# Routing of a mixture of experts: the last tile ahead of the 0/1 products, picks ahead of the destinations, the second half's picks in two pieces

## What is computed

```python
xf = x.reshape(T, D)                       # T = 1024 rows, D = 512, after a layer norm
logits = xf @ gate_w.T                     # 8 experts
probs = softmax(logits)
top_p, top_i = top_k(probs, 2)
w = top_p / (sum(top_p) + 1e-09)
capacity = int(1.25 * T / 8)               # 160 rows of each of the two choices per expert
oh = one_hot(top_i, 8)
rank = cumsum(oh, axis=0) - 1
keep = sum(rank * oh, -1) < capacity
comb = einsum('tk,tke->te', w * keep, oh)
for e in range(8):
    y = (silu(xf @ gate_proj_w[e].T) * (xf @ up_proj_w[e].T)) @ down_proj_w[e].T
    out = out + comb[:, e:e+1] * y
```

## Time and profile before

| what | us |
|---|---|
| median of 3 runs | 1009.5 |
| lowest and highest run | 1008.39, 1009.78 |
| the profiled execution | 1006.8 |
| its span, first to last instruction | 1005.1 |

### The profile page before, as it was taken

How to read it: one execution, slowest core, us unless ns; L and a number is a source line. 1 busy time by engine, 2 the same in 40 slices (tenths; PEclk the granted TensorE clock), 3 DMA queues, 4 the chain that set the end, 5 groups by cost and what they waited for, 6 DMA issues and landing times.

```text
span 1005.1 us, 14411 instructions
## 1 busy us (share of the span) xinstructions
PE 985.9 (98%) x5412; PEld 777.0 (77%) x5412; DVE 614.8 (61%) x1142; ACT 393.7 (39%) x631; POOL 215.9 (21%) x202
## 2 busy tenths in 40 slices
PE   7999999999999999999999999899999999999998
PEld 4886444445454468878888887899999999999997
DVE  6368443344655565896466668577665666656666
ACT  3332211222111143355667542444544444445441
POOL 2053400002000036454422124720000000000051
PEclk9999999999999999999999999999999999999999
DMA  9809599999999922033311100885764756645543
GB/s 295 317 1 381 241 361 417 409 414 397 415 396 408 388 94 74 1 92 108 110 42 38 32 1 7 277 283 156 217 188 151 206 159 196 189 155 183 152 150 133
DMA packets 45959, 206.91 MB, mean 206 GB/s; under 512 B 5760, under 2 KB 16256, under 8 KB 41680
## 3 DMA queue, kind: packets, MB, share of 16 engines
q1 hardware_dynamic: 40256, 187.95, 52.6%
q0 software_dynamic: 5648, 18.22, 5.4%
HBM read 190.04 MB, written 16.12 MB: 205 GB/s over the span
## 4 chain that ended last, share of the span: by engine, by line
PE 85%; DVE 7%; DMA 6%; issue 1%; ACT 0%; SPq 0%; POOL 0%; DVEq 0%; ACTq 0%
PE ps L486 59%; PE ps L621 7%; PE ps L650 7%; DMA big<-in_ctxT 3%; DMA big<-in_ctx 2%; DVE stats L1315 2%; PE ps L480 2%; PE ps L598 1%; PE ps L951 1%; PE ps L856 1%; PE ps L978 1%; PE ps L654 1%; PE ps L631 1%; PE ps L493 1%; DVE hr L1324 1%; PE ps L532 1%
## 5 line engine op out<-in xcount | busy, mean ns | idle before, releaser
L486 PE MATMUL ps<-x,w 128*128 128x320 f32 x1536 | 235.6, 309 | 0.0
L486 PEld LDWEIGHTS ps<-x,w 128*128 128x128 f32 x1536 | 228.0, 188 | 0.4
L1839 DVE TENSOR_TENSOR w<-big,w 128x1536 fp32r<-128x1536 f32 x64 | 112.1, 1753 | 78.3 <-ACT w L1249 78.3
L486 PE MATMUL ps<-hsplit,w 128*128 128x320 f32 x672 | 107.7, 309 | 0.0
L1249 ACT CAST w<-big 128x1536 fp32r<-128x1536 f32 x64 | 94.2, 1475 | 29.2 <-PE ps L486 27.0
L486 PEld LDWEIGHTS ps<-hsplit,w 128*128 128x128 f32 x672 | 100.8, 188 | 0.1
L486 PE MATMUL ps<-xcT,u 128*128 128x512 f32 x432 | 98.2, 389 | 0.0
L621 PE MATMUL ps<-big 128*64 128x512 f32 (+2 forms) x512 | 95.9, 500 | 0.7 <-DVE s_stat L1495 0.6
L486 PEld LDWEIGHTS ps<-xcT,u 128*128 128x128 f32 x432 | 81.0, 188 | 17.0 <-DVE xcT L1627 0.2
L650 PE MATMUL ps<-big 128*64 128x512 f32 x384 | 86.4, 597 | 1.7 <-DMA big<-in_ctx 1.5
L621 PEld LDWEIGHTS ps<-big 128*64 128x64 f32 x512 | 44.2, 136 | 51.0 <-issue 39.1
(11 more groups left out here) (336 smaller groups left out, 1544.6 us busy)
## 6 DMA issues: line engine op xcount, KB each, us to landing
big<-in_ctxT SPq DMA_DIRECT2D x16, 3202.0 KB, 19.3
big<-in_ctx SPq DMA_DIRECT2D x16, 3072.0 KB
big<-in_w_units SPq DMA_DIRECT2D x64, 768.0 KB, 4.4
big<-in_dense_units SPq DMA_DIRECT2D x41, 256.0 KB, 2.7
xs<-big POOLq DMA_DIRECT2D x1, 5120.0 KB, 17.4
big<-in_gate_units SPq DMA_DIRECT2D x12, 384.0 KB, 3.0
hr<-xs SPq DMA_DIRECT2D x28, 160.0 KB, 5.8
ys<-big POOLq DMA_DIRECT2D x28, 160.0 KB, 5.6
```

The lines of the kernel that those rows point to most:

```text
L486: mm = nc.tensor.matmul(dst, lhs[x], rhs[w], start=start and x + w == 0, stop=stop and x == 1)
L1839: V.tensor_tensor(wsplit[f % RING][1][:], wraw[f % RING], wsplit[f % RING][0][:].bitcast(F32), ALU.subtract).then_inc(w_low, 1)
```

## The change

PE's order behind the last output chunk changes: the first quarter of the first half's rows goes ahead of tile 5's logits; tile 6's logits, and `ranks_before`, go behind the transposition of tile 7; tile 7's logits follow tile 6's at once. The second half's products are made in two rounds over the four quarters, tiles 4 and 5 in the first, 6 and 7 in the second, instead of all four tiles for each quarter.

On DVE the slot within the first expert no longer comes out of `scat`'s chain: `one_hot` adds one sum (L1747 of the new file, `rt[:, 7]`), `positions` ends with one sum of the rank and that (`rt[:, 1]`), and the picks compare with it. The four instructions that lead to `scat` are a function `destinations` of their own behind the picks. The cut at the capacity isn't in the picks' numbers; a rank over the capacity gives a number that no slot of its choice has. The second half's picks are two instructions of two tiles each. `one_hot(0)` moves ahead of tile 5's `last_apply`. On ACT the last two instructions of the stretch change places.

```diff
-            def first_expert_rows(d, h):
-                pe.wait_ge(picked, h + 1)
-                if h == 0:
+            def first_expert_rows(d, q):
+                pe.wait_ge(picked, q + 1)
+                if q == 0:
                     wait_bank_free(pe, "gx", d)
-                for i in range(4 * h, 4 * h + 4):
+                for i in range(*((0, 4), (4, 6), (6, 8))[q]):
                     pe.wait_ge(row_low, i + 1)
...
-                if h:
+                if q == 2:
                     mm.then_inc(xt_done if d else gx_done, 1)
...
             output_chunks(7, 5, HC)
+            first_expert_rows(0, 0)
             logits(1, 5, 4, 6)
-            first_expert_rows(0, 0)
             transposed_tiles(6, 7)
-            ranks_before()
-            logits(1, 6, 4, 6)
             first_expert_rows(1, 0)
             transposed_tiles(7, 8)
+            logits(1, 6, 4, 6)
+            logits(2, 7, 7, 7)
             first_expert_rows(2, 0)
-            logits(2, 7, 7, 7)
+            ranks_before()
+            ranks_within(1)
             first_expert_rows(3, 0)
-            ranks_within(1)
-            for d in range(DC):
-                first_expert_rows(d, 1)
+            for q in (1, 2):
+                for d in range(DC):
+                    first_expert_rows(d, q)
...
             last_transposed(6)
+            last_transposed(7)
             rows_high(7)
-            last_transposed(7)
...
+                rt_chained(V.tensor_tensor(rt[:, 7, n], rt[:, 2, n], slot_at[:, 1, n], ALU.add))
...
                 rt_chained(V.tensor_reduce(rt[:, 3, n], rk[:, n, :], AX_X, ALU.add))
+                rt_chained(V.tensor_tensor(rt[:, 1, n], rt[:, 3, n], rt[:, 7, n], ALU.add))
+
+            def destinations(h):
+                _, n = half_tiles(h)
                 rt_chained(V.tensor_tensor(rt[:, 5, n], rt[:, 3, n], rt[:, 2, n], ALU.add))
...
             choose(0, 0, 4)
+            one_hot(0)
             last_apply(5)
-            one_hot(0)
             last_norm(6)
             positions(0)
             last_apply(6)
             dve.wait_ge(slots_in, 16)
-            pick_rows(0)
+            pick_rows(0, 4)
+            destinations(0)
             last_norm(7)
             last_apply(7)
             choose(1, 4, 7)
             choose(2, 7, 8)
             one_hot(1)
             positions(1)
-            pick_rows(1)
+            pick_rows(4, 6)
+            pick_rows(6, 8)
+            destinations(1)
```

More of the change, by code:

```diff
@@ L958, in transpose_picks @@
             def transpose_picks(i):
-                pe.wait_ge(picked, 3 + NT // 2)
+                pe.wait_ge(picked, 4 + NT // 2)
                 if i == 0:
@@ L1759, in positions, with pick_rows @@
                 V.tensor_copy(scat[:, n], rt[:, 4, n]).then_inc(idx_done, 1)
[L1761 to L1765, removed]
+            def pick_rows(lo, hi):
+                ids = slot_ids.rearrange("p (k s) -> p k s", s=CAP).unsqueeze(1).to_broadcast([P, hi - lo, TOPK, CAP])
+                V.tensor_tensor(pick[:, lo:hi, :].rearrange("p i (k s) -> p i k s", s=CAP), ids,
+                                r3[1][:, lo:hi, :].unsqueeze(3).to_broadcast([P, hi - lo, TOPK, CAP]),
                                 ALU.is_equal).then_inc(picked, 1)
```

## The result

The changed kernel takes 1003.91 us (median of 5 runs, 1002.8 to 1004.43), the kernel before 1008.9 (5 runs, 1008.39 to 1009.78). The ratio is 0.9947, 95% interval 0.9932 to 0.9962: some 5 us faster, 3.8 to 6.9. The prediction was 1006.4, and its range began at 1004.6: the direction was right, the gain was over one and a half times the forecast, and the time lies outside the range.

A forecast was written before the change was run, and what follows sets the result against it. It took DVE and PE alternating in the second half's routing as the bound. Experts starting 4.1 us earlier, cut to 3.1 by late rows, gave 1003.7 profiled, plus 2.7 to the median: 1006.4 us, range 1004.6 to 1008.9.

The forecast's parts named there:

- What bounds it, and that the rest passes the gain on: Second half's routing alternates between DVE and PE; afterwards PE waits only 0.4 us, so gains reach the end unless expert 0 intervenes.
- The front: First half's comparison ahead of tile 5's apply: 0.25 us gained of PE's 0.79 us wait, bounds 0 and 0.79.
- PE up to the ranks: PE's reordered work before the second half's ranks: they start at 637.2 instead of 638.55 us, bound by PE, not DVE.
- From the ranks to the experts: First picks end at 639.95, products take 4.7 us at full clock; experts start at 644.7 instead of 648.78, 4.1 us earlier.
- The scatters: POOL's 16 scatters: first at 636.0 instead of 634.5, holds of 6 us, last start at 660.9, 2.4 us later.
- the reading by which DVE's weight instructions hold no scatter: Alternative reading of POOL's holds: last scatter would start near 655 and the whole 4.1 us would stay.
- What expert 0 gives back: Last scatter lands in 4.3 us (bounds 3.6 and 6.6), expert 1's rows come at 670.6, leaving a 3.1 us gain.
- DVE's wait of 1 us at the turn: DVE reaches the turn of expert 1's rows at 669.6, but they come at 670.6; this wait isn't hidden.
- the sign of misread scatters: The stated test at the turn of expert 1's rows: if DVE doesn't wait there, the scatters were misread.
- The median carried over: The profiled execution was 2.7 us under the 1009.5 median; that difference was added to 1003.7, giving 1006.4.
- The sum: Whole kernel: 3.1 us gain however early the experts start, profiled execution 1006.8 to 1003.7, median forecast 1006.4.
- the rows come in time: Rival, chance 0.25: expert 1's rows arrive by 669.6, the whole 4.1 us stay, up to 4.7; 1004.8 to 1005.4.

The follow-up runs named there:

- without PE's order: Changed kernel with PE's and ACT's orders as in the kernel before; tile 3's logits to the experts' first product took 29.90 us, 26.72 in the changed kernel.
- two at a time alone: Kernel before with only the second half's picks split into two-tile pieces and its products in two rounds; tile 3's logits to experts' first product 30.75 us, 31.42 before.
- before, PE kept busy: Kernel before with 18 unused products added on PE during its wait for the second half's picks; tile 3's logits to experts' first product 29.95 us, 31.42 before.
- picks first alone: Kernel before with only the picks ahead of the destinations and the two added sums; tile 3's logits to experts' first product 30.93 us, 31.42 before.
- three more moves: Changed kernel with an output chunk ahead of first-half ranks, two third-quarter tiles behind second-half ranks, tile 0's scatters ahead of `row7low`; 1002.77 us.
- PE's order alone: Kernel before with only the new orders on PE and ACT; tile 3's logits to the experts' first product 29.74 us, 31.42 before.
- without the early comparison: Changed kernel with `one_hot(0)` behind tile 5's apply again; tile 3's logits to the experts' first product 27.06 us, 26.72 in the changed kernel.
- without two at a time: Changed kernel with the second half's picks one instruction and its products one round again; tile 3's logits to experts' first product 27.36 us, 26.72 in the changed kernel.
- last scatter held, shorter: Changed kernel, last scatter held until DVE made the sixth slice's low weights; tile 3's logits to seventh slice's down products 68.56 us, 65.5 in the changed kernel.
- last scatter held, longer: Changed kernel, last scatter held until DVE split the fourth slice's hidden values; tile 3's logits to seventh slice's down products 70.85 us, 65.5 in the changed kernel.
- without picks first: Changed kernel with the picks behind the destinations again, without the two added sums; tile 3's logits to experts' first product 27.17 us, 26.72 in the changed kernel.

## Why the prediction was wrong, step by step

- **What bounds it, and that the rest passes the gain on:** right. PE waits for nothing but 0.4 us from the experts' start to the end, as before.
- **The front:** right within 0.15. The comparison was held under `row4low`, as said (1.26 us at L1744 instead of 0.22), and PE's wait went from 0.79 to 0.40: 0.39 instead of the forecast 0.25, 0.34 by the run without it. The Trainium skill has this in "SBUF — State Buffer", section "Who interferes with whom": two SBUF inputs on VectorE contend with a GpSimd instruction that reads SBUF. The trace agrees.
- **PE up to the ranks:** the order was right, the size was not. The ranks start 2.0 us earlier (21.2 to 19.15 us behind tile 3's logits), and I had 1.35. I had priced sets by the distance of starts in the profile before, where each changed to another kind of product: the first quarter took 1.17 us (630.43 to 631.60) instead of 1.26, tile 5's logits 0.80 instead of 0.91, and the logits of tiles 6 and 7 ran as one set of 1.75, where I had 1.62 for a wait and 0.8 for a set.
- **From the ranks to the experts:** right. 2.77 us to the first product of tiles 4 and 5 (forecast 2.75, from 637.2 to 639.95), 4.80 at full clock (4.7). The experts start 4.7 us earlier instead of 4.1.
- **The scatters:** right but for the start. The first starts 1.0 us later, not 1.5, since tile 7's transposition came sooner than I had it; the holds add up to 6.0 us (43.01 - 18.15 - 18.9), as forecast. The last starts 1.9 us later, not 2.4. So the reading by which DVE's weight instructions hold no scatter, which put the last start near 655, is out: the scatter at 652.94 took 2.34 us beside such an instruction (652.69 to 654.45). Why they hold one, no run here shows; the rule quoted for it in the prediction speaks of GpSimd instructions that read SBUF.
- **What expert 0 gives back: this step failed**, and it made the largest part of the miss. I took 4.3 us for the landing of the last scatter, with 3.6 as the lower bound, the shortest in the earlier trace rows. It took 2.8. The rows were there 2.1 us earlier than before, counted from tile 3's logits, and not 0.1 later: 1.5 of these 2.2 us are the landing, 0.5 the scatter's start, 0.2 the load. DVE's wait of 1 us at the turn didn't come, which is the sign of misread scatters that I had named. The reason that I gave for a short landing fits the runs, and I didn't follow it to its end: counted from tile 3's logits, the weights of the eighth slice were asked for 4.7 us earlier (35.3 instead of 40.0) and had landed when the last scatter started. The 3.6 was the wrong bound, since no scatter of the profile before had both no weights in flight and no scatter behind it: the one without weights, the fifth, started at 639.7 and landed in 4.2 with others ahead of it and behind. The runs line up on this (from issue and landing times; the start of the last scatter is counted from the landing of those weights):

| kernel | start against the weights' landing, us | landing took, us |
|---|---|---|
| without PE's order | -6.8 | 7.1 |
| before | -6.2 | 6.6 |
| two at a time alone | -5.2 | 6.2 |
| before, PE kept busy | -5.2 | 6.1 |
| picks first alone | -4.4 | 5.6 |
| three more moves | -2.8 | 4.3 |
| PE's order alone | -1.7 | 3.3 |
| without the early comparison | 0.0 | 2.9 |
| the whole change | +0.2 | 2.8 |
| without two at a time | +0.4 | 2.7 |
| last scatter held, shorter | +3.2 | 3.0 |
| last scatter held, longer | +5.7 | 2.7 |

  In the run without picks first the start is -0.1, and the landing is not in its trace; SP, which waits for it, issued its load 2.7 us after the start. That is twelve executions in one line, not a test in which the weights alone were moved, so that the weights are the cause is argued and not shown. By the Trainium skill, "DMA: Bandwidth & Descriptors", section "Anatomy of one DMA — SWDGE (gpsimd) path", such a DMA takes 2.0 us and the bytes at 436 GB/s; for 256 KB that is an estimate of 2.6, and the trace agrees for a last scatter behind the weights' landing, with 2.7 to 3.0.
- **The median carried over:** the kernel before has 1008.9 with five runs, where three had given 1009.5.
- **The sum:** the miss of 2.5 us is 1.0 for a wait that didn't come, 0.6 for the experts' earlier start, 0.6 for the median, and 0.3 that is within the scatter of the runs. The first two hang on the same step: by my sum the gain was 3.1 however early the experts start, and without a wait at the turn their whole 4.7 stayed. The rival "the rows come in time" is what happened. It was priced with the same start that was too late, at 1005.4, 1004.8 at best, and so the range, which ended just below it, was too narrow. Its condition was also off by my own terms: a landing of 3.6 puts the rows at 669.9 (660.9 + 3.6 + 5.4), not at 669.6.

## What to carry to other kernels

An idle time of PE behind which the granted clock falls is worth more than its length, and the clock's part belongs to no single edit: cost the edits together, and one by one see whether the clock still falls. When work moves earlier, ask of every transfer behind it what shared its queues before and whether that is still there; the shortest landing in a trace is no lower bound for a transfer that will have less beside it than any there. Compare executions from the last common point ahead of the change, since the runs differ by more in front of it than small edits are worth.

## What the runs showed of the hardware that I had not expected

In this stretch the granted clock stayed at 1.00 behind 0.50, 0.98 and 1.17 us of idle time, and went to 0.50 (1.2 GHz) behind 1.63, 1.70, 2.17, 2.37 and 2.84. Right ahead of the wait stand the ranks' products of 16 to 64 columns where PE's order is the old one (1.70 and more), and eight products of 320 columns where it is the new one (1.63 and less). Each such fall cost the 32 products behind it some 1.5 us (6.32 to 6.33 instead of 4.79 to 4.81). The length of the wait alone doesn't decide: with the shorter hold PE waited 1.79 us in expert 0, between products of 320 columns, and the granted clock stayed at 1.00; the longer hold's 3.60 us brought it to 0.50. What makes the difference stays open. An indirect scatter of 256 KB landed between 2.7 and 8.8 us after its start (the longest in the version with three more moves); for the last of the 16 this goes with how far the weights' load still reaches into it, as the table above shows.
